# Two-block transformer, mixture-of-experts tiles: expert weights copied to fixed buffers by VectorE, f32 matmuls with fixed addresses, second bias added on the tokens' side

## The reference

```python
logits = x @ gate_w + gate_b            # x: 2048 tokens x 128, 8 experts
topw, topi = top_k(softmax(logits), K)  # K = 2, then 1, 1
hid = act(einsum('nd,edf->enf', x, w1) + b1)     # 128 -> 512
out = einsum('enf,efd->end', hid, w2) + b2       # 512 -> 128
y   = sum over the chosen experts of topw * out
x   = x_residual + y
```

## Time and profile before

| | us |
|---|---|
| median of 3 timed runs | 1203.41 |
| lowest, highest | 1202.26, 1234.69 |
| profiled execution, its own time | 1192.77 |
| its span, first to last instruction | 1190.6 |
| granted TensorE clock, mean share of full | 0.819 |
| PE busy | 846.7 (71%) |
| DVE busy | 674.1 (57%) |
| ACT busy | 507.5 (43%) |
| POOL busy | 226.8 (19%) |

### The profile page before, as it was taken

One profiled execution on the slowest core, in us unless ns is written; L12 is line 12 of the kernel. 1 busy time (PEld: TensorE's weight loads), 2 busy tenths in 40 slices (PEclk: granted clock), 3 DMA queues, 4 the chain that ended last, 5 costly groups with the idle time before them and its releaser, 6 DMA issues.

```text
span 1190.6 us, 17358 instructions
## 1 busy us (share of the span) xinstructions
PE 846.7 (71%) x5666; PEld 481.4 (40%) x5666; DVE 674.1 (57%) x1340; ACT 507.5 (43%) x1061; POOL 226.8 (19%) x208
## 2 busy tenths in 40 slices
PE   4599644888825547898878888878784787574784
PEld 2377434666614331111111111111564565374663
DVE  6734767111157768669999999960626311574112
ACT  1110431433316353458888888884233233211332
POOL 2000014465511200000000000000302464101562
PEclk9799756899967765559999999995795699785798
DMA  6100210111120000000000000000203111101113
GB/s 161 46 1 1 72 35 10 35 43 41 41 80 1 0 1 1 1 1 1 1 1 1 1 1 1 1 1 1 71 1 106 27 41 37 35 1 35 39 43 93
DMA packets 35946, 32.98 MB, mean 28 GB/s; under 512 B 6898, under 2 KB 28738, under 8 KB 35874
## 3 DMA queue, kind: packets, MB, share of 16 engines
q1 hardware_dynamic: 30434, 20.82, 6.1%
q0 software_dynamic: 5440, 11.15, 3.7%
HBM read 22.18 MB, written 9.76 MB: 27 GB/s over the span
## 4 chain that ended last, share of the span: by engine, by line
PE 44%; DVE 17%; issue 10%; ACT 10%; POOL 8%; another core or an unknown queue 5%; DMA 3%; SPq 2%; DVEq 0%; POOLq 0%; ACTq 0%
PE psum L1331 12%; PE psum L1319 9%; ACT arena L1383 6%; POOL results L891 4%; POOL arena L883 3%; DVE arena L1298 2%; DVE stats L158 2%; PE psum L1283 2%; PE psum L217 2%; PE psum L916 2%; PE psum L934 2%; PE psum L1449 1%; DVE xn L186 1%; PE psum L282 1%
## 5 line engine op out<-in xcount | busy, mean ns | idle before, releaser
L1298 DVE TENSOR_REDUCE arena<-psum 128x2 f32<-128x1024 f32 x256 | 300.2, 1219 | 48.8 <-PE psum L1283 47.4
L1383 ACT ACTIVATE arena<-psum 128x512 f32<-128x512 f32 x512 | 264.6, 604 | 108.5 <-PE psum L1319 108.4
L1319 PE MATMUL psum<-arena 32*128 32x512 f16 x512 | 130.0, 425 | 60.7 <-ACT arena L1383 59.5
L1018 ACT ACTIVATE arena<-psum,e_b 128x128 f32<-128x128 f32 x340 | 96.4, 370 | 157.2 <-remote 120.3
L1331 PE MATMUL psum<-arena 128*32 128x512 f32 x1024 | 157.0, 690 | 0.0
L1145 DVE TENSOR_TENSOR arena<-psum,arena 128x128 f32 (+1 forms) x85 | 24.8, 292 | 206.1 <-remote 148.6
L1283 PE MATMUL psum<-arena 32*128 32x512 f16 x512 | 122.1, 429 | 12.1 <-DVE arena L1298 9.1
L1319 PEld LDWEIGHTS psum<-arena 32*128 32x128 f16 x512 | 30.3, 92 | 247.8 <-ACT arena L1383 217.3
L970 PE MATMUL psum<-arena,expert_w 128*128 128x128 f16 x1020 | 99.5, 239 | 35.2 <-ACT arena L1018 31.3
L981 PE MATMUL psum<-expert_w,arena 128*128 x680 | 104.6, 299 | 2.3 <-issue 1.3
L891 POOL DMA_INDIRECT results<-arena x85 | 83.6, 984 | 92.2 <-DVE arena L1145 77.2
(11 more groups left out here) (246 smaller groups left out, 1112.5 us busy)
## 6 DMA issues: line engine op xcount, KB each, us to landing
arena<-results SPq DMA_DIRECT2D x16, 256.0 KB, 4.1
tokens<-arena SPq DMA_DIRECT2D x6, 512.0 KB, 3.2
arena<-in_L_attn_b_w_dram SPq DMA_DIRECT2D x1, 2048.0 KB, 8.5
arena<-in_L_ffn_W_dram SPq DMA_DIRECT2D x1, 2048.0 KB, 9.4
arena<-tokens,arena POOLq DMA_INDIRECT x85
results<-arena POOLq DMA_INDIRECT x85
x<-in_L_attn_a_x_dram SPq DMA_DIRECT2D x2, 512.0 KB, 5.3
out_dram<-x SPq DMA_DIRECT2D x1, 1024.0 KB, 5.1
```

The costliest lines, as they stand in the source:

```text
L1018: last = nc.scalar.activation(self.hT[:, p, c, :], ps[:, 2 + p, c * P:(c + 1) * P], self.func, bias=self.ew.b1[:, c:][:, bass.ds(at, 1)])
L1298: v.tensor_reduce(self.mx[:, h % 2, keys, qt, 2 * pair:2 * pair + 2], core.psum[:, 2 * slot:2 * slot + 2, :], AX.X, ALU.max).then_inc(self ...
L1319: nc.tensor.matmul(core.psum[:, 4 + tile % self.SCORE_BANKS, :], self.kT[rows, g, at:at + P], self.qT2[rows, h % 2, :], start=True, stop=T ...
L1383: nc.scalar.activation(self.prob[:, k % self.PROBS, j, :], core.psum[:, 4 + tile % self.SCORE_BANKS, :], ACT.Exp).then_inc(self.prob_in, 1)
```

## The change

It removes the f16 parts of tokens and first-layer weights. Tokens go to DRAM as f32 straight from `xn`. One array of 8 x 1028 f32 holds w1, b1 and w2 of each expert; it is loaded in one go (w1 by one DMA, b1 by one, w2 by eight) at the place of `load_w2`. For each tile DVE loads the expert's offset into a register and copies the 1028 columns to one of four fixed buffers (`own`), one tile ahead; PE and ACT then use fixed addresses. The first layer is 4 f32 matmuls per tile. The loops of ACT and DVE are written out. The third bf16 bias matmul is gone; instead a matrix of token weights per expert (`wh`, 128 x 128) is transposed on PE, copied by ACT to `whT`, and four f32 matmuls of 32 rows by 512 columns with `b2_blocks` give the bias of all tokens, which DVE adds to `x` before its first tile. `b2_blocks` is made at the start of the kernel by `bias_blocks`, out of `b2` loaded 16 times to 8 partitions each.

```diff
+EW = FF + FC + FC * D
...
-        self.expert_w = self.sb("expert_w", [P, 2 * NE * FF])
+        self.expert_w = self.sb("expert_w", [P, NE * EW])
...
-        w.e0.split_biases(dve)
-        w.e1.split_biases(dve)
+        w.bias_blocks(dve)
...
-        self.e0.load_w2(sp)
+        self.e0.load(sp)
...
-        for e in (self.e0, self.e1):
-            e.bias_to_rows(sp)
-        for e in (self.e0, self.e1):
-            sp.wait_ge(e.rows_in, e.rows_all)
-        sp.wait_ge(self.arena_free, 1)
-        self.e0.load_w1(sp)
...
+    def bias_blocks(self, dve):
+        core, v = self.core, self.core.nc.vector
+        core.vstep(v.tensor_reduce(self.of_row[:, :], self.ident[:, :].rearrange("p (t e) -> p t e", e=NE), AX.X, ALU.add))
+        core.vstep(v.tensor_reduce(self.of_tile[:, :], self.of_row[:, :].rearrange("p (g j) -> p j g", j=4), AX.X, ALU.add))
+        for e in (self.e0, self.e1):
+            dve.wait_ge(e.small_in, e.small_all)
+            v.tensor_tensor(e.b2_blocks[:, :, :], e.b2_rows[:, :].unsqueeze(1).to_broadcast([P, 4, D]),
+                            self.of_tile[:, :].unsqueeze(2).to_broadcast([P, 4, D]), ALU.mult).then_inc(e.blocks_in, 1)
...
-        loads = [(self.gate[:, :], d["gate"]), (self.gate_b[:, :], d["gate_b"].partition_broadcast(P)),
-                 (self.b1[:, :], d["b1"]), (self.bias_wide[:, :], d["b2"])]
+        loads = [(self.gate[:, :], d["gate"]), (self.gate_b[:, :], d["gate_b"].partition_broadcast(P))]
+        loads += [(self.b2_rows[NE * t:NE * (t + 1), :], d["b2"]) for t in range(T)]
...
-    def round_w1(self, act):
...
-    def split_w1(self, eng, k):
...
-    def bias_to_rows(self, sp):
...
-    def split_biases(self, dve):
...
+    def load(self, sp):
+        d, parts = self.from_dram, self.parts
+        sp.dma_start(parts[:, :, 0:FF], d["w1"].rearrange("e p f -> p e f")).then_inc(self.weights_in, 16)
+        sp.dma_start(parts[:, :, FF:FF + FC], d["b1"].rearrange("p (e c) -> p e c", e=NE)).then_inc(self.weights_in, 16)
+        for e in range(NE):
+            sp.dma_start(parts[:, e, FF + FC:].rearrange("p (c d) -> p c d", c=FC),
+                         d["w2"][e].rearrange("(c p) d -> p c d", p=P)).then_inc(self.weights_in, 16)
...
+        self.own, at = c(core, at, [self.HELD, EW])
+        self.sorted, at = c(core, at, [tiles, D])
...
-        for b in range(B):
-            ts = slice(b * TB, (b + 1) * TB)
-            pool.wait_ge(self.rounded, b + 1)
-            g_.tensor_tensor(self.split16[:, ts, D:2 * D], core.xn[:, ts, :], self.split16[:, ts, 0:D],
-                             ALU.subtract).then_inc(self.parts_in, 1)
...
-        if self.fresh:
-            self.ew.split_w1(g_, 1)
...
-        pe.wait_ge(self.ew.w1_split, 2)
-        pe.wait_ge(self.ew.w2_in, 16)
-        pe.wait_ge(self.ew.rows_in, self.ew.rows_all)
-        pe.wait_ge(self.tables_in, 2)
-        pe.wait_ge(w.ones_rows_in, 1)
-        pe.wait_ge(w.ident16_in, 1)
-        w1, w2, brows = self.ew.w1_parts, self.ew.w2, self.ew.bias_rows
-        column = {}
+        core.claim(pe, self.turn)
+        pe.wait_ge(self.turned, 1)
+        nc.tensor.transpose(ps[:, self.turn.bank, 0:P], self.wh.rearrange("p t e -> p (t e)"),
+                            w.ident[:, :]).then_inc(core.filled[self.turn.bank], 1)
+        core.moved(pe, self.turn)
+        pe.wait_ge(self.ew.blocks_in, 1)
+        for g, turn in enumerate(self.bias):
+            core.claim(pe, turn)
+            rows = slice(32 * g, 32 * g + 32)
+            nc.tensor.matmul(ps[:, turn.bank, :], self.whT[rows, :], self.ew.b2_blocks[rows, :, :],
+                             start=True, stop=True).then_inc(core.filled[turn.bank], 1)
         for s in range(self.tiles + 3):
-            t = s - 1
-            if 0 <= t < self.tiles:
-                column[t] = self.tile_value(pe, 0, slice(t, t + 1), (NE - 1) * FF)
             t = s
             if t < self.tiles:
                 p, m = t % 2, t // 2
                 pe.wait_ge(self.tile_in[p], 16 * m + 16)
-                if t < 2:
-                    self.claim(pe, 0, p, m)
-                for k in range(2):
-                    last = nc.tensor.transpose(ps[:, p, k * 64:(k + 1) * 64].bitcast(F16),
-                                               self.sorted16[:, t, k * D:(k + 1) * D], w.ident16[:, :])
-                last.then_inc(core.filled[p], 1)
+                self.claim(pe, 0, p, m)
+                nc.tensor.transpose(ps[:, p, 0:P], self.sorted[:, t, :], w.ident[:, :]).then_inc(core.filled[p], 1)
             t = s - 1
             if 0 <= t < self.tiles:
                 p, m = t % 2, t // 2
+                own = self.own[:, t % self.HELD, :]
                 self.moved(pe, 0, p, m)
                 self.claim(pe, 1, p, m)
+                pe.wait_ge(self.copied, t + 1)
                 for c in range(FC):
-                    for i, (of_w, of_x) in enumerate(((0, 0), (0, 1), (1, 0))):
-                        last = nc.tensor.matmul(ps[:, 2 + p, c * P:(c + 1) * P],
-                                                w1[:, of_w, c * P:][:, bass.ds(column[t], P)], self.xgT[:, p, of_x, :],
-                                                start=(i == 0), stop=(i == 2))
+                    last = nc.tensor.matmul(ps[:, 2 + p, c * P:(c + 1) * P], own[:, c * P:(c + 1) * P],
+                                            self.xgT[:, p, :], start=True, stop=True)
                 last.then_inc(core.filled[2 + p], 1)
             t = s - 3
             if t >= 0:
                 p, m = t % 2, t // 2
+                own = self.own[:, t % self.HELD, FF + FC:]
                 self.moved(pe, 1, p, m)
                 self.claim(pe, 2, p, m)
-                at = column.pop(t)
                 for c in range(FC):
-                    nc.tensor.matmul(ps[:, 4 + p, 0:D], self.hT[:, p, c, :], w2[:, c * D:][:, bass.ds(at, D)],
-                                     start=(c == 0), stop=False)
-                nc.tensor.matmul(ps[:, 4 + p, 0:D], w.ones_rows[:, :], brows[:, bass.ds(at, D)],
-                                 start=False, stop=True).then_inc(core.filled[4 + p], 1)
-    def tile_value(self, eng, which, tile, largest):
-        return eng.value_load(self.tile_at[0:1, which, tile], min_val=0, max_val=largest)
+                    last = nc.tensor.matmul(ps[:, 4 + p, 0:D], self.hT[:, p, c, :], own[:, c * D:(c + 1) * D],
+                                            start=(c == 0), stop=(c == FC - 1))
+                last.then_inc(core.filled[4 + p], 1)
...
-        for b in range(B):
-            ts = slice(b * TB, (b + 1) * TB)
-            act.wait_ge(self.normed, b + 1)
-            nc.scalar.copy(self.split16[:, ts, 0:D], core.xn[:, ts, :]).then_inc(self.rounded, 1)
...
-        act.wait_ge(self.tables_in, 2)
-        def step(s, p, m):
-            at = self.tile_value(act, 1, slice(s, s + 1) if s is not None else bass.ds(2 * m + p, 1), (NE - 1) * FC)
-            if s is None or s >= 2:
+        core.result(act, self.turn)
+        nc.scalar.copy(self.whT, ps[:, self.turn.bank, 0:P]).then_inc(core.emptied[self.turn.bank], 1)
+        for t in range(self.tiles):
+            p, m = t % 2, t // 2
+            own = self.own[:, t % self.HELD, :]
+            if t >= 2:
                 self.used_before(act, 2, p, m)
             self.result(act, 1, p, m)
             for c in range(FC):
                 last = nc.scalar.activation(self.hT[:, p, c, :], ps[:, 2 + p, c * P:(c + 1) * P], self.func,
-                                            bias=self.ew.b1[:, c:][:, bass.ds(at, 1)])
+                                            bias=own[:, FF + c:FF + c + 1])
             last.then_inc(core.emptied[2 + p], 1)
-        self.over_tiles(act, step, 0)
...
-        if self.fresh:
-            self.ew.split_w1(v, 0)
+        v.tensor_scalar(self.tile_at[0:1, 0, 0:n], off, float(EW), None, ALU.mult).then_inc(self.tables_in, 1)
+        weight = self.top_p[:, 0, :].unsqueeze(2).to_broadcast([P, T, NE])
+        first = v.tensor_tensor(self.wh, self.hot[:, 0, :, :], weight, ALU.mult)
+        if self.top == 2:
+            core.vmark(first)
+            weight = self.top_p[:, 1, :].unsqueeze(2).to_broadcast([P, T, NE])
+            core.vstep(v.tensor_tensor(tmp, self.hot[:, 1, :, :], weight, ALU.mult))
+            first = v.tensor_tensor(self.wh, self.wh, tmp, ALU.add)
+        first.then_inc(self.turned, 1)
...
+        for g, turn in enumerate(self.bias):
+            xs = core.x[:, 4 * g:4 * g + 4, :]
+            core.result(dve, turn)
+            v.tensor_tensor(xs, xs, ps[:, turn.bank, :].rearrange("p (t d) -> p t d", d=D),
+                            ALU.add).then_inc(core.emptied[turn.bank], 1)
+        dve.wait_ge(self.ew.weights_in, self.ew.weights_all)
+        dve.wait_ge(self.tables_in, 1)
+        def take_weights(t):
+            at = dve.value_load(self.tile_at[0:1, 0, t:t + 1], min_val=0, max_val=(NE - 1) * EW)
```

(31 more changed lines are left out.)

105 lines of the change are left out of this document (21 added, 84 removed).

## The result

| | before | after |
|---|---|---|
| median of the timed executions, us | 1203.45 (4) | 1169.59 (4) |
| lowest, highest | 1202.26, 1234.69 | 1157.16, 1183.84 |
| profiled execution, its span | 1190.6 | 1157.5 |
| granted TensorE clock, mean | 0.819 | 0.832 |

The ratio is 0.963 (95% interval 0.960 to 0.966): the change makes the kernel faster, by over three times what I forecast (0.989), and I gave a time under 1179 us a chance of 0.25 only. Executions of one kernel on one chip differ by up to 7%, and every ratio with an interval in this document compares the faster executions of the two kernels. The profiles show where they differ: one stage that the change doesn't touch, the softmax attention's loop, runs for a varying time at TensorE's lower level of 1.2 GHz; this has to be taken out before the rest can be read.

A forecast was written before the change was run, and what follows sets the result against it. It took the tile loops to be held by the handshake of ACT and PE, neither full. Terms +10.3 - 4.7 - 3.9 + 7.6 - 22.2 = -12.9 from 1192.8 gave 1179.9 profiled, median 1190 us, own range 1180 to 1202.

The forecast's parts named there:

- The frame: Whole kernel: profiled forecast 1179.9 us times 1.0089 gives the median, 1190; no term for the attention's loop.
- Around the loops: Start, routing and bias, all that lies around the tile loops: sum +9.3 us (+2 to +19).
- Start: Kernel start: 36 small loads instead of eight delay DVE's wait and so L379, +10.3 us (9 to 13).
- Splitting goes: Routing before each loop: without POOL's splitting, DVE's steps run unhindered, -4.7 and -3.9 us.
- Bias: Before tile 0 of each block: computing the tokens' bias adds 5.3, 1.0 and 1.3 us, together +7.6.
- Loops: Three tile loops: ACT's 4.2 us hold goes, POOL becomes the bound at 3.0 us a tile, -22.2 us.
- Rival D: Tile loops: the pairwise wait of ACT stays, period 3.25 us a tile, median 1213; chance 7%.
- rival C: Tile loops: TensorE's clock falls to 1.2 GHz for half the tiles, PE becomes the bound, median 1243; chance 13%.
- Rival B: Tile loops: every DVE copy adds its whole time to POOL, 3.26 us a tile, loops 239.6, median 1207; chance 25%.
- 3.38 a tile: Tile loops: by the skill's page, DVE's copy blocks POOL wholly, 3.38 us a pair, estimated time 1214 us.

The follow-up runs named there:

- the push: 24 extra f16 matmuls of 128 rows by 512 columns before and among the attention loop's first scores; medians 1173.7 us (kernel before) and 1151.5 (changed kernel).
- the filling: 21 extra f16 matmuls of 128 rows by 512 columns between PE's first attention score pieces; medians 1192.4 us (kernel before) and 1177.5 (changed kernel).
- b1: The kernel before with 24 extra f16 matmuls before and among the first scores of the attention's loop; median 1173.7 us.
- b2: The changed kernel with 24 extra f16 matmuls before and among the first scores of the attention's loop; median 1151.5 us.
- d1: The kernel before with the push, again, on another chip with late completions; median 1174.1 us, profiled span 1171.9.
- d2: The changed kernel with the push, on that same other chip with late completions; median 1159.6 us, profiled span 1149.2.
- a3: The changed kernel once more, unedited; 1151.7 to 1168.7 us, ratio 0.990 to the kernel before.
- e1: The changed kernel again, unedited; 1156.9 us against 1186.0 of the kernel before, ratio 0.988.
- b4: The changed kernel without the tokens' bias (output lacks the second bias); first gather to first `y` took 12.5, 10.9 and 10.4 us.
- b3: The changed kernel without DVE's weight copies and their register loads, every tile taking a fixed expert's weights; tile loops 223.7 us.
- c1: The changed kernel with `bias_blocks` on DVE moved behind the first block, on another chip; 1138.1 us, tile loops 206.9.
- c4: The changed kernel with bias blocks behind the first block, one more step between transpose and first layer, and the push; median 1144.9 us, ratio 1.000.
- e3: The changed kernel with DVE's step ordered copy of tokens, next weights, `y`, and five held buffers; 1151.7 to 1198.1 us, tile loops 227.8.
- e2: The changed kernel with bias blocks behind the first block and the push, on a fifth chip; 1150.9 us, ratio 0.960 to the kernel before.
- a1: The kernel before with 21 extra f16 matmuls between PE's first score pieces of the attention; median 1192.4 us.
- a4: The kernel before with the tile loops of ACT and DVE written out; 1166.6 to 1212.6 us, tile loops 236.9.

## Why the prediction was wrong

The sum of the steps against six profiles of the changed kernel and four of the kernel before, all on chips with late completions (means, us; three profiles of each kernel have the push or the filling, and their part ahead of the attention's loop adds 3 to 4 us):

| step | forecast | measured |
|---|---|---|
| start, L379 | +10.3 | +7.3 |
| to the first gather (splitting goes) | -8.6 | -5.1 - 5.3 - 2.1 = -12.5 |
| first gather to first `y` (the bias) | +7.6 | +3.2 - 1.4 - 1.7 = +0.1 |
| tile loops | -22.2 | 244.9 to 227.8 = -17.1 |
| other stages outside the attention | 0 | -1.6 (-0.5 to -1.0 between like profiles) |
| sum outside the attention's loop | -12.9 | 825.2 to 801.7 = -23.5 |
| attention's loop, first pair of profiles | 0 | -17.2 |

- **The frame, a step that failed.** I carried the median over by one factor, 1.0089, as if the executions differed evenly, and put the attention's loop at nothing. It stood in the profile of before with a clock of 0.5 for 70 us, PE busy 90% in most of it, and its length went from 346 to 388 us over the profiles. A sum of single microseconds was set on a base that moves by 60; the forecast should have named this stage and priced it. It made the measured ratio 0.963 out of an effect of about 0.98 (1151.5 to 1173.7 in b1 and b2, 1149.2 to 1171.9 in the profiles of d1 and d2) or 0.99 (a3, e1). By the ratios of a3 and e1 alone my 0.989 would have been met; by the stages it was missed, with 23.5 us outside the attention's loop instead of 12.9.
- **Around the loops, the other step that failed.** I had +9.3 there (+2 to +19) and -6.4 was measured, outside my bounds. The next three terms make up 14 of these 16 us, and the loops, which gained 5 less than forecast, hide a part of them.
- **Start.** Mechanism right, mis-sized: the b2 loads are issued 0.34 to 0.37 us apart (5.40 and 5.93 for 16), not 0.38, and the last released DVE in 1.5, not 3.15. The 3.15 was that of the first expert's four loads together. In the kernel before the second expert's last load, issued at 20.31, had its last update at 22.46, 1 us before DVE came to it: eight small operations held L379 there, and not this load.
- **Splitting goes.** Right in kind, as far as the stages show (no run puts the splitting back alone): -12.5 instead of -8.6. The term of the first block was a guess (-1.2): its four L1103 took 10.59 before and take 6.72 now, -3.9, and the first of these two rows could have been read beforehand.
- **Bias.** The first block came out as forecast (5.5 by b4, against 5.3). In the other two I charged 2.3 us and it is hidden. What remains, 1.4 to 2.3 us less to the first `y` in each block, is a gain that I didn't see; b4 shows that it isn't the bias, and I have no run that shows which part of the first tiles it is.
- **Loops.** The time a tile came near (3.0 named, 3.1 measured), but by luck, and the step that failed in the mechanism is "so what held ACT for 4.2 us should go. [...] The bound is then POOL". It did not go (37.6 us of such waits in 100, up to 4.0 each), and POOL isn't the bound (b3). What held ACT is that PE's completions reach it up to some 4.7 us late. I had put the wait down to the register loads; the row said "remote", which is to say that the view didn't know. Rival D was that the wait stays; it stays in part. On the chip of c1 to c4 POOL is the bound, with partial sharing, as the forecast had it.
- **Clock in the loops** (rival C): 0.92 to 0.94. It stood at 0.5 for 34 of the 232 us, more than before (15 of 245) and far from half. It doesn't set the pace: e3 had 14 us at 0.5 and took 227.8, a3 had 41 and took 226.5.
- **Rival B**, 239.6 us in the tile loops, is out on both kinds of chip (227 and 207). So is the estimate worked out by the Trainium skill's page "SBUF — State Buffer", 3.38 a tile.
- Two slips in the prediction change nothing: POOL is busy 58% in the earlier trace rows, not 59%, and the sum with 3.38 comes to 1215, not 1214.

## What to carry to other kernels

Before summing small terms, look for a stage whose clock sits at the lower level while PE is busy: its length varies from one execution to the next, by more here (42 us) than the whole change, and it is to be cut out of each trace before two kernels are compared. A wait with an unknown releaser is an open question, not a term that goes when the suspect nearest to it goes. The same kernel can be bound by something else on another chip: compare kernels on one chip.

## What the runs showed of the hardware

- Chips differ: the same kernel before took 1165.9 to 1180.3 us at its shortest on three chips, 1187.7 on a fourth (e2), and 1131.5 on the one of c1 to c4. In the four profiles of that chip PE's completions in the tile loops are recorded within 0.02 us of its end, and the tile loops of the same code were 20 us shorter (206.9 against 227). In the 16 profiles on the others, 41 to 104 of some 231 completions in the tile loops come over 1 us late and in bunches, and none over 0.5 outside them; DVE's own are recorded 0.01 us after its end in the same stretch (223:320 of the changed kernel). All of c1 to c4 were measured together, so that it is the chip, and not the occasion, rests on the chip of a1 to a4, which had the late ones each of three times.
- What holds them back I have not found. It is not the hardware loops (a4), nor the weight copies (b3), nor DVE's order (e3), nor the clock (e3 against a3), nor gathers alone, since 7 of them fly ahead of each first `y` with no late completion. In the two profiles of the first pair late ones begin within 3 us after each loop's first scatter; no run without scatters was made, and on the chip of c1 to c4 the same scatters bring none.
- Whether the change gains anything on such a chip stays open: no profile of the kernel before was taken there. c4, with the push and two more edits, has the ratio 1.000 to it, and c1, with 5.5 us less at the first gather and an attention's loop of 361 us, took 1138.1, within the executions of before (1131.5 to 1197.5). Both speak for little or nothing; that is argued, not shown.
- At the start of the attention's loop, whose matmuls have 32 rows or 32 columns, the clock stayed at 1.2 GHz in the 14 profiles without the push, with PE busy 90% (475:525 of the kernel before), and rose some 23, 62, 70, 78, 102 or 140 us after the first exponential. In all six profiles with the push, 24 matmuls of 128 rows by 512 columns, it stood at 1.0 by then; in c4 and e2 it fell back to 0.5 some 27 and 31 us after it had risen, for 92 and 48 us.
- In every profile the clock also falls to 0.5 near the end of that loop, in the kernel before at 803.6 with the last exponential at 827.0, in the changed kernel at 791.3 with the last at 810.7. So even the shortest loops, of 346 us, have such a stretch.
